# Attention kernel: seven PSUM banks divided four and three between two rotations, or three and four

## The reference

```python
x = L0_attn_x                                   # (8, 1024, 256), 16 heads of 16, latent width 32
q, k, v = heads of (x @ c_attn_w.T + c_attn_b)
q_lat, k_lat, v_lat = q @ q2l_w.T + q2l_b, k @ kv2l_w.T + kv2l_b, v @ kv2l_w.T + kv2l_b
q_lat, k_lat = rope(q_lat), rope(k_lat)         # t * cos + rotate_half(t) * sin
q_for_k = q_lat @ wqk_w.T + wqk_b
att = softmax(where(causal, q_for_k @ k_lat.T * 32 ** -0.5, -inf))
y = (att @ v_lat) @ l2o_w.T + l2o_b             # then the output projection
x = layernorm(x + y @ cproj_w.T + cproj_b)
x = layernorm(x + experts(x))
```

## Time and profile before

| | |
|---|---|
| median of 3 runs | 2509.27 us (2500.8 to 2524.76) |
| profiled execution, its own time | 2506.28 us |
| its span, first to last instruction | 2504.6 us |
| mean granted clock of TensorE in it | 0.912 |
| busy: PE, DVE, ACT, POOL | 2162.4, 1672.8, 1366.1, 1373.5 us |

### The profile page before, as it was taken

One profiled execution on the slowest core, in us unless ns is written; L12 is line 12 of the kernel. 1 busy time (PEld: TensorE's weight loads), 2 busy tenths in 40 slices (PEclk: granted clock), 3 DMA queues, 4 the chain that ended last, 5 costly groups with the idle time before them and its releaser, 6 DMA issues. The chain is left out here.

```text
span 2504.6 us, 43646 instructions
## 1 busy us (share of the span) xinstructions
PE 2162.4 (86%) x12268; PEld 1490.6 (60%) x12268; DVE 1672.8 (67%) x4866; ACT 1366.1 (55%) x3316; POOL 1373.5 (55%) x1606
## 2 busy tenths in 40 slices
PE   2698998999899999899899899940999999996876
PEld 2454655555555555556556566430888888885665
DVE  2476687686577687677677678434777777773676
ACT  0155655555545565564564566621677777773333
POOL 1455465664654754763674675415566666665562
PEclk7799999998898898998998999865999999998898
DMA  3556556556545555564565565250222222223563
GB/s 116 129 123 146 120 119 155 113 120 142 124 100 133 118 130 136 120 136 120 125 131 128 119 128 129 49 199 7 65 71 71 71 71 70 70 71 105 158 185 114
DMA packets 192967, 284.06 MB, mean 113 GB/s; under 512 B 55752, under 2 KB 113760, under 8 KB 192608
## 3 DMA queue, kind: packets, MB, share of 16 engines
q1 hardware_dynamic: 173664, 238.18, 40.0%
q0 software_dynamic: 16768, 34.69, 4.8%
q10 hardware_dynamic: 2304, 8.39, 0.9%
HBM read 99.41 MB, written 37.56 MB: 55 GB/s over the span
## 5 line engine op out<-in xcount | busy, mean ns | idle before, releaser
L515 ACT ACTIVATE probs<-scores_T 128x512 f32<-128x512 f32 (+3 forms) x1536 | 654.5, 492 | 258.5 <-PE scores_T L405 245.9
L748 POOL TENSOR_SCALAR_AFFINE_SELECT probs<-probs 128x256 f32<-128x256 f32 x512 | 205.6, 410 | 544.4 <-ACT probs L515 541.7
L463 PE MATMUL ring<-k_stack,q_stack_b 96*128 96x512 f32 (+3 forms) x1024 | 403.5, 437 | 19.4 <-DVE neg_part L660 9.1
L660 DVE TENSOR_REDUCE neg_part<-ring 128x1 f32<-128x512 f32 x512 | 333.2, 683 | 96.5 <-PE ring L463 93.5
L405 PE MATMUL scores_T<-q_stack_b,k_stack 98*128 98x512 f32 (+3 forms) x1024 | 328.3, 398 | 46.5 <-ACT probs L515 45.8
L422 PE MATMUL o_ps<-probs,v_ones 128*17 128x512 f32 (+3 forms) x3072 | 350.7, 530 | 1.9 <-POOL probs L748 1.7
L463 PEld LDWEIGHTS ring<-k_stack,q_stack_b 96*128 96x128 f32 x1024 | 196.7, 201 | 228.9 <-issue 84.8
L665 DVE CUSTOM_DVE_ANT_0 ring<-ring,mask 128x384 f32<-128x384 f32 (+3 forms) x512 | 243.3, 507 | 116.7 <-PE ring L463 114.5
L665 DVE CUSTOM_DVE_ANT_0 ring<-ring,mask,neg_part 128x384 f32<-128x384 f32 (+3 forms) x512 | 260.7, 554 | 83.6 <-PE ring L463 83.3
L1076 ACT ACTIVATE o_sb<-ht_ps,ln_b,ln_g 128x128 f32<-128x128 f32 x544 | 217.1, 449 | 114.7 <-PE ht_ps L1024 76.4
L405 PEld LDWEIGHTS scores_T<-q_stack_b,k_stack 98*128 98x128 f32 x1024 | 193.3, 206 | 104.0 <-ACT probs L515 79.5
(11 more groups left out here) (192 smaller groups left out, 4682.2 us busy)
## 6 DMA issues: line engine op xcount, KB each, us to landing
u_rot<-u SPq DMA_DIRECT2D x128, 256.0 KB, 3.7
k_stack<-u_rot SPq DMA_DIRECT2D x128, 256.0 KB
y_rows<-z SPq DMA_DIRECT2D x136, 128.0 KB
lat_w<-lat_split SPq DMA_DIRECT2D x32, 512.0 KB
q_stack_a<-u_rot SPq DMA_DIRECT2D x64, 256.0 KB
q_stack_b<-u_rot SPq DMA_DIRECT2D x64, 256.0 KB
k_stack<-u SPq DMA_DIRECT2D x64, 256.0 KB
x_raw<-in_xT SPq DMA_DIRECT2D x16, 512.0 KB, 4.9
```

The costliest lines, as they stand in the source:

```text
L463: nc.tensor.matmul(out[:, 0:k1 - k0], q_stack[qb // 4][0:3 * L, row_buf(n, qb // 4), h, P * (qb % 4):P * (qb % 4) + P], k_stack[0:3 * L, n ...
L515: nc.scalar.activation(probs[:, s % 2, h, cols], sc[(t + j) % 3][:, HALF - w:HALF], ACT.Exp).then_inc(exp_done, 1)
L660: nc.vector.tensor_reduce(neg_part[:, n % 2, part_col], src[:], AX_X, ALU.max, negate=True).then_inc(max_taken, 1)
L748: nc.gpsimd.affine_select(both, both, [[0, 2], [1, P]], ALU.is_ge, zero, base=0, channel_multiplier=-1).then_inc(kept, 1)
```

## The change

The ring gets three banks and the transposed scores four. So PE may write a ring item once the item three places back is freed, and a block of transposed scores once the exponential four blocks back is done. The readers (`scalar_items`, `vector_items`, `route_step`) take the bank from the same rotation. Nothing else is different: the instructions of each engine, their order, shapes and number are the same in both kernels.

```diff
-        ring = [ctx.enter_context(nc.psum_tensor(f"ring{i}", [P, HALF], F32)) for i in range(4)]
-        sc = [attention.enter_context(nc.psum_tensor(f"scores_T{i}", [P, HALF], F32)) for i in range(3)]
+        ring = [ctx.enter_context(nc.psum_tensor(f"ring{i}", [P, HALF], F32)) for i in range(3)]
+        sc = [attention.enter_context(nc.psum_tensor(f"scores_T{i}", [P, HALF], F32)) for i in range(4)]
...
-                    out = ring[place % 4]
-                    if place >= 4:
-                        pe.wait_ge(*freed(ring_users[place - 4]))
+                    out = ring[place % 3]
+                    if place >= 3:
+                        pe.wait_ge(*freed(ring_users[place - 3]))
...
-                        if t + j >= 3:
-                            pe.wait_ge(exp_done, t + j - 2)
-                        nc.tensor.matmul(sc[(t + j) % 3][:, HALF - w:HALF], k_stack[:, n % 2, h, P * kb:P * kb + P],
+                        if t + j >= 4:
+                            pe.wait_ge(exp_done, t + j - 3)
+                        nc.tensor.matmul(sc[(t + j) % 4][:, HALF - w:HALF], k_stack[:, n % 2, h, P * kb:P * kb + P],
...
-                        nc.scalar.activation(probs[:, s % 2, h, cols], sc[(t + j) % 3][:, HALF - w:HALF],
+                        nc.scalar.activation(probs[:, s % 2, h, cols], sc[(t + j) % 4][:, HALF - w:HALF],
```

More of the change, by code:

```diff
@@ L506, in scalar_items @@
                     place = ring_place[it]
-                    src = ring[place % 4]
+                    src = ring[place % 3]
                 if kind == "B":
@@ L602, in route_step @@
                                                ALU.subtract)
-            counts = ring[ring_place["CNT", b] % 4]
+            counts = ring[ring_place["CNT", b] % 3]
             if i == 13:
@@ L641, in vector_items @@
                     cols = slice(HALF * part, HALF * part + HALF)
-                    src = ring[ring_place["WQ", n, part] % 4]
+                    src = ring[ring_place["WQ", n, part] % 3]
                     dve.wait_ge(q_hi_ready, 2 * n + part + 1)
```

## The result

The changed kernel has a median of 2541.2 us (8 runs, 2532.91 to 2544.01) against 2505.03 for the kernel before (8 runs). One of those eight took 4977 us; the ratio leaves it out. The ratio is 1.0138, 95% interval 1.0103 to 1.0174: 1.4% slower, some 35 us. The forecast was 1.7% slower. A repeat in another set of runs gave 1.0162 (1.0117 to 1.0207). Profiles of different sets are compared in the attention alone.

What follows compares the result with a forecast made beforehand. Engines waiting for each other in fixed order, decoupled by banks, were taken to bound the attention. 2506.3 + 73 - 30 = 2549 us; with the median 3.0 us higher, forecast 2552 us, 1.7% slower, range 2475 to 2625.

Steps and rivals of the forecast that it cites:

- What bounds the kernel: Attention: no engine is full (DVE 69%); engines wait for each other in fixed order, and the banks decouple them.
- The matmuls' view: PE's waits counted at matmuls in the attention: 47.0 us for exponentials, 13.3 for DVE's reductions; by it a gain.
- the loads' view: PE's waits counted at weight loads in the attention: 95.6 us for exponentials, 151 for reductions; by it a loss.
- the faster rival: Attention: score bank frees 47.0 us of matmul waits, ring's 13.3 at most double; 2475 us, chance 0.18.
- the long holds: Seven PE waits at line 405, 4.4 to 5.8 us; to reappear at line 463 shorter by 1.5 to 2 us.
- Term 1: Attention's ring loses a bank, so S items wait one DVE reduction longer: 73 us loss, bounds 0 and 259.
- The count of 259 us: Summed lateness of 611 ring items starting before the item three back is freed, each counted alone; taken as ceiling.
- Term 2: Attention's scores gain a bank, so waits for exponentials go: 30 us gain (12 plus 18), bounds 11 and 95.6.
- The rival "nothing": POOL's rotation of the keys paces the attention's units, swallowing loss and gain: 2490 to 2529 us, chance 0.22.
- Much slower: Attention: PE's ring delays add up through ACT and KH to DVE, 150 to 200 us; 2630 to 2680, chance 0.10.
- The signs: Attention: loads' exponential waits under 15 us, reduction waits 250 to 400 in over 450; DVE dry time up by the loss.
- The clock: Granted clock, 0.92 over the attention, could fall or rise; given no term, left to the range.

Runs made afterwards that it cites:

- three and three: Three banks for the ring and three for the scores, eighth bank unused, against the kernel before: ratio 1.0212 (1.0174 to 1.025), 52 us slower.
- the last of the POOL runs: Kernel before with POOL's bias addition moved to place 13.75 and its scaling of y_T to 37.4: ratio 1.0064 (1.0035 to 1.0093).
- six shared: One rotation of six banks for ring items and scores in TensorE's order, against the kernel before: ratio 0.9902 (0.9883 to 0.9922).
- seven shared: One rotation of seven banks for ring items and scores in TensorE's order, against the kernel before: ratio 0.9878 (0.9828 to 0.9928).
- first POOL move: POOL's bias addition moved from place 10.75 to 13.75: ratio to the kernel before 1.006 on that kernel, 1.030 on the changed one.
- five and two: Five banks for the ring and two for the scores, against the kernel before: ratio 1.0036 (1.0015 to 1.0057).
- by who frees: Changed kernel's three and four banks, redivided: what ACT frees turns through the four, what DVE frees through the three; ratio to the kernel before 1.005 (1.0018 to 1.0081).
- five shared: One rotation of five banks for ring items and scores in TensorE's order, two unused, against the kernel before: ratio 1.0229 (1.018 to 1.0278).
- four and two: Four banks for the ring and two for the scores, one unused, against the kernel before: ratio 1.0148 (1.0106 to 1.019), 37 us slower.
- four and three: The kernel before the change, with four banks for the ring and three for the scores: median 2505.03 us, ratio 1.

## Why the prediction was right, and where not

**What bounds the kernel** held: no busy time moved, and the attention alone took the loss.

**Which view to go by** held. The matmuls' view had forecast a gain (2475 us), the loads' view a loss, and it was a loss. The matmuls' waits for reductions ahead of S did not double, as the faster rival had it, but went from 13.3 to 44.7 + 11.8 = 56.5 us. Over half of that are the long holds, which came back at line 463 as forecast, so the rival's doubling left out what the prediction itself expected. The Trainium skill, Perfetto Trace Analysis, section "Identifying the Most-Contended Engine", prefers the loads for judging how busy TensorE is; it speaks of busy time, and the carrying over to waits was the prediction's own step. The sign of this change agrees with it.

**Term 1** had the right sign and was too large: 73 us forecast, 2.1% or 52 us measured by three and three. The count of 259 us was rightly not taken as it stood, but my way of thinning it, by DVE's backlog, still gave 40% too much. Its mechanism was half right. The dry time of DVE rose by 24.5 us and that of ACT by 20.8; I had put it all on DVE and named ACT only as what the count left out. And about two thirds of the net loss went away when ACT's holders left the ring's rotation, while term 1 was written as DVE's reductions alone. It also took each reduction to end one reduction later; where KL stands between, it was up to 3.4 us later.

**Term 2** was too large as well: 30 us forecast, 12 to 18 measured. The waits for exponentials did go, as forecast (under 15 us; 14.6). The seven holds did move to line 463 behind one step of PV, but only three got shorter, by 1.6 to 2.5 us, and the seven together by 4 us: KL, whose length the prediction did not count, took 2.3 to 3.4 us in the other four. (Two times in the prediction are misread: in the kernel before the first of these waits ends at 248.1 us and the last at 1419.6, not at 252.5 and 1425.1. Nothing else rests on them.) That I gave the holds 12 us of worth is not supported: moving POOL's work out of them made them short and the kernel no faster, though what was moved had its own price elsewhere.

**The sum** of 43 us against 35 came out near partly by luck: both terms were a third or more too high, and one is taken from the other. It is the terms' difference that was tested by the result; the terms by the experiments.

**The rival "nothing"**, POOL's rotation paces the units, falls with the result itself, a loss of 1.4% with an interval that starts above 1.0%. The last of the POOL runs speaks against it too: ACT's wait for the rotation went from 102.0 to 31.3 us and the time rose by 0.6%. **"Much slower"** needed 150 us. **The signs** given: loads' waits ahead of S at 250 to 400 us in over 450 waits, measured 243.5 in 414, just below; DVE's dry time up by about the loss, measured by two thirds of it. **The clock** rose from 0.92 to 0.94 in the attention, so it did not make the loss; what it may have given back is not known.

What stays open is why six shared banks nearly equal seven shared and five fall off by 3%. The experiments show that six or seven banks in one rotation beat seven divided; beyond the long holds they don't say where the sharing pays.

## What to carry to other kernels

When two producers' rotations share a fixed number of banks and one engine issues both in a fixed order, try one rotation for all before shifting a bank from one to the other: here shifting cost 1.4% one way and 0.4% the other, and sharing gained 1.2%, or 1.0% with one bank to spare. Where banks must be divided, try dividing by the engine that frees them: here that got back about two thirds of a loss. A large repeated wait is not a price, nor is the consumers' dry time: ask of each wait what is ready right behind it. And when work is moved on one engine, look at what now runs beside it on the others: here KL went from 0.69 to 4.3 us, and no count of instructions shows that.

## What the runs showed of the hardware that was not expected

**An operation on DVE that lasts as long as one on POOL.** KL (line 651) takes 0.69 us in most of its 64 times. Over 2 us it took, in the timelines of the kernels before and changed, of three and three and of the first POOL move, only where POOL's scaling of y_T (line 754, 2.4 us) or its bias addition (line 757, 4.5 us) ran beside it. Beside the addition it took 4.3 us and ended half a microsecond after it, fourteen times out of fourteen. Why these two hold each other was not tried.

**Two durations of one stage.** The last stage, which gathers rows by indirect DMA, took one of two times with the same instructions. The first and last starts of its products, in the kernel before and in the repeat of the changed kernel:

```profile
L1218 PE MATMUL f_ps<-y,diag x256: 376/379/793, 2294.4 to 2489.7; 128*128 128x256 f32 x128
```

```profile
L1218 PE MATMUL f_ps<-y,diag x256: 379/379/634, 2330.8 to 2485.0; 128*128 128x256 f32 x128
```

195 us against 154, so 41 us: more than the change itself. It goes with the set of runs and not with the kernel. It is not the chip's number alone either: chip 9 was used for two sets, and the stage took 154 us in the first (five and two, six shared) and 194 to 197 in the second (by who frees, five shared), with medians of 2462 and 2500 us for the kernel before. So a time from one set must not stand beside one from another. What makes it was not tried.

**More banks.** Within the division a bank more helped: three and three took 1.021 and four and two 1.015 of the time of four and three. But how the banks were divided counted for as much. The Trainium skill, Perfetto Trace Analysis, section "Matmul Optimizations", asks that all eight banks be used; here six shared and one for the output, seven in all, beat the eight of the kernel before, 0.9902 (0.9883 to 0.9922), and the eighth gained nothing beyond the intervals (0.9878, 0.9828 to 0.9928).
